# Many-headed attention: scores ahead of the transposed scores, banks exchanged, and queries of two batches in one product

## The chip, the cores and the metric

The kernel runs on one core of a Trainium2 chip. Its engines work side by side and wait for each other only through semaphores: TensorE (PE: products and transposes, written to PSUM; its loads of the stationary operand are listed as PEld), VectorE (DVE), ScalarE (ACT), GpSimd (POOL) and SyncE (SP, which here only issues DMAs). PSUM has eight banks. The metric is the time of one execution on the device in microseconds; the median of several executions is compared.

## The reference

The program is a stack of four gated blocks, each with a cross attention and a feed-forward part, over 32 batches of 112 queries with 256 features and a context of 375 rows. The change touches the cross attention of the third block:

```python
# L2_xattn: 16 heads of 16 features; q = layernorm(x), k = v = ctx
qh = (q @ Wq.T + bq).reshape(B, 112, 16, 16).transpose(0, 2, 1, 3)
kh = (k @ Wk.T + bk).reshape(B, 375, 16, 16).transpose(0, 2, 1, 3)
vh = (v @ Wv.T + bv).reshape(B, 375, 16, 16).transpose(0, 2, 1, 3)
scores = einsum('bhqd,bhkd->bhqk', qh, kh) / sqrt(16)
scores = where(key_padding_mask, scores, -inf)
out = einsum('bhqk,bhkd->bhqd', softmax(scores), vh)
x = x + tanh(g_xattn[2]) * (out.reshape(B, 112, 256) @ Wo.T + bo)
```

## The kernel before

`many_headed_attention` (L2686) computes this attention for 32 batches. A unit is four heads, so a batch has four units and the stage has 128 (n = 4j + u for batch j, unit u). All engines walk the same loop over n from FIRST to LAST. One turn of it is called a slot here; in slot n each engine does what is due for several units at once, in an order fixed by the code.

What happens to a unit:
1. `scores(n)` (L3053, slot n): four heads at once, each on 32 rows of TensorE, 112 queries by 375 keys, written to banks 0 to 3 (SCORE).
2. `find_top(n, h)` on VectorE (L2842), once for each of the four heads: adds the mask and takes the top of each row. `logits_done` counts these.
3. `transpose_top(n)` (L3061, slot n+1) turns the tops, and `extend_q(n)` on VectorE (L2850, slot n+1) writes them into a spare row of the queries, so that the next product comes out with the top subtracted.
4. `scores_t(n)` (L3031, slot n+3): the same scores, transposed, three pieces of 125 keys for four heads, written to banks 4 to 7 (SCORE_T).
5. `exp(n)` on ScalarE (L2935, slot n+3): three instructions for head 0 (bank 4), then three for the other three heads. `probs_done` counts them.
6. `attend(n)` (L3073, slot n+3): probabilities by values.

TensorE does two more things in a slot, each in a bank that the scores leave free for a while.
- The front operation uses bank 4 before the change (FRONT = SCORE_T). It is `transpose_raw` (L3084) in slot u=0, `transpose_att` (L3091) in u=1, `project_out` (L3098) in u=2 and `project_q` of the next batch (L3108) in u=3. It has to wait until the three exponentials of head 0 have read bank 4: `front_free` waits for `probs_done`.
- The back operation uses bank 0 (BACK = SCORE). It is `project_k` (L3120) for half of the next batch's keys in u=0 and u=2, `project_v2` (L3127) with `transpose_xn` (L3133) in u=1, and `project_v01` (L3141) in u=3. `back_free` waits for the first `find_top` of the slot.

Who empties these banks: ScalarE copies keys (L2952), values (L2962, L2966), normalised rows (L2942), raw results (L2973) and `att_t` (L2979); VectorE does `norm_att` (L2855, L2862), `residual` (L2872) and `mask_q` (L2827), which spreads the projected queries of one batch into `q_t` with two instructions.

The order of TensorE in a slot before the change is: transposed scores of n-3, scores of n, front operation, back operation, `transpose_top(n-1)`, `attend(n-3)`. The order of VectorE is: `find_top` for heads 0, 1 and 2, what empties the front operation, `find_top` for head 3, `extend_q(n-1)`, then statistics for a later batch.

Of the kernel before, what the change touches and what calls it, by code (L numbers as in the profile page):

```python
# [13 lines left out]
P = 128  # L14
# [2671 lines left out]
def many_headed_attention(k, w, f):  # L2686
# [3 lines left out]
    with nc.cleanup_on_exit():  # L2690
        V_HOMES = 3
# [11 lines left out]
        xn_t = sb(nc, "xn_t", [P, DC, S], F32)  # L2703
        q_t = sb(nc, "q_t", [P, 2, DC, PARITIES, S], F32)
# [17 lines left out]
        FRONT, BACK = SCORE_T, SCORE  # L2722
# [3 lines left out]
        FIRST, LAST = -UNITS, N + UNITS + 3  # L2726
# [15 lines left out]
        with nc.Block() as block:  # L2742
# [14 lines left out]
            def _(pool):  # L2757
# [30 lines left out]
                norm(0)  # L2788
                mask(0)
# [4 lines left out]
                for n in range(FIRST, LAST):  # L2794
                    j, u = divmod(n, UNITS)
                    if u == 1 and j + 2 < B:
                        norm(j + 2)
# [14 lines left out]
            def _(dve):  # L2812
# [7 lines left out]
                def mask_q(j):  # L2820
                    dve.wait_ge(s["q_done"], j + 1)
                    if j == 0:
                        dve.wait_ge(w.s["scale_ready"], 1)
                    if j >= 2:
                        dve.wait_ge(s["scores_t_done"], UNITS * (j - 1))
                    for a in range(DC):
                        ins = dve.scalar_tensor_tensor(q_t[:, j % 2, a, :, :], k.ps[:, FRONT, a * S:(a + 1) * S].unsqueeze(1).broadcast_to([P, PARITIES, S]),  # L2827
                                                       w.bq[:, a:a + 1], w.q_scale.unsqueeze(2).broadcast_to([P, PARITIES, S]), ALU.add, ALU.mult)
                    ins.then_inc(s["q_masked"], 1)
# [15 lines left out]
                def extend_q(n):  # L2845

                    j, u, a, parity = unit(n)
                    q = q_t[:, j % 2, a, parity, :]
                    dve.wait_ge(s["top_transposed"], n + 1)
                    dve.scalar_tensor_tensor(q, TOP, other[:, parity:parity + 1], q, ALU.mult, ALU.add).then_inc(s["q_extended"], 1)  # L2850
# [23 lines left out]
                statistics(0)  # L2874
                dve.wait_ge(w.s["narrowed"], 2)
# [20 lines left out]
                for n in range(FIRST, LAST):  # L2896
                    j, u = divmod(n, UNITS)
                    if 0 <= n < N:
                        find_top(n, 0)
                        find_top(n, 1)  # L2900
                        find_top(n, 2)
                    if u == 0 and 0 <= j - 2 < B:
                        norm_att(j - 2)
                    if u == 2 and 0 <= j - 2 < B:
                        residual(j - 2)
                    if u == 3 and j + 1 < B:
                        mask_q(j + 1)
# [4 lines left out]
                    if u == 1 and j + 2 < B:  # L2912
                        statistics(j + 2)
                    if u == 2 and 0 <= j - 2 < EARLY:
                        dve.wait_ge(s["residual_done"], j - 1)
                        ternary_statistics(k, f, dve, j - 2)
                    if u == 1 and j == 6:
                        dve.wait_ge(f.s["rows_loaded"], 48)
                        dve.tensor_scalar(f.scale[:, :], f.scale[:, :], 1e-5, None, ALU.max).then_inc(f.s["scale_cut"], 1)
                        dve.wait_ge(f.s["scale_cut"], 1)  # L2920
                        dve.reciprocal(f.inv_scale[:, :], f.scale[:, :]).then_inc(f.s["inverted"], 1)

            @block.scalar
            def _(act):
# [13 lines left out]
                def copy_xn(j):  # L2938
                    act.wait_ge(s["xn_transposed"], j + 1)
                    if j:  # L2940
                        act.wait_ge(s["q_done"], j)
                    act.activation(xn_t[:, :, :], k.ps[:, BACK, D:D + DC * S].rearrange("p (a t) -> p a t", a=DC), ACT.Copy).then_inc(s["xn_t_copied"], 1)  # L2942
# [12 lines left out]
                def copy_v2(j):  # L2955
                    act.wait_ge(s["v2_done"], j + 1)
                    act.wait_ge(s["xn_transposed"], j + 1)
# [22 lines left out]

                for n in range(FIRST, LAST):
                    j, u = divmod(n, UNITS)
                    if 0 <= n - 3 < N:
                        exp(n - 3, 0, 1)
                        exp(n - 3, 1, UNIT)
                    if 0 <= n - 4 < N:
                        copy_raw(n - 4)
                    if u == 1 and 0 <= j - 2 < B:
                        copy_att_t(j - 2)
                    if u == 0 and j + 1 < B:  # L2990
                        copy_k(j + 1, 0)
                    if u == 1 and j + 1 < B:
                        copy_v2(j + 1)
                        copy_xn(j + 1)
# [6 lines left out]
            def _(pe):  # L3001
                def front_free(n):

                    if 0 <= n < N:
                        pe.wait_ge(s["probs_done"], EXPS * n + KC)

                def back_free(n):

                    if 0 <= n < N:
                        pe.wait_ge(s["logits_done"], UNIT * n + 1)  # L3010

                def scores_t(n):
                    j, u, a, parity = unit(n)
                    b, v = divmod(n + 3, UNITS)
# [5 lines left out]
                    if v == 0:  # L3020
                        pe.wait_ge(s["q_masked"], min(b + 1, B))
                    if v == 1 and b >= 2:
                        pe.wait_ge(s["att_normed"], b - 1)
                    if v == 2 and b >= 2:
                        pe.wait_ge(s["att_t_copied"], b - 1)
                    if v == 3 and b >= 2:
                        pe.wait_ge(s["residual_done"], b - 1)
                    for r in range(KC):
                        for h in range(UNIT):
                            rows = slice(h * VW, (h + 1) * VW)  # L3030
                            mm = pe.matmul(k.ps[0:KR, SCORE_T + h, r * S:(r + 1) * S], k_t[rows, j % 2, a, parity, r * KR:(r + 1) * KR],  # L3031
                                           q_t[rows, j % 2, a, parity, :], start=True, stop=True)
                    mm.then_inc(s["scores_t_done"], 1)

                def scores(n):
                    j, u, a, parity = unit(n)
                    pe.wait_ge(s["q_masked"], j + 1)
# [5 lines left out]
                    if u == 0:  # L3043
                        pe.wait_ge(s["v01_copied"], j + 1)
                    if u == 1:
                        pe.wait_ge(s["k_copied"], min(DC * (j + 1) + 1, DC * B))
                    if u == 2:
                        pe.wait_ge(s["xn_t_copied"], min(j + 2, B))
                    if u == 3:
                        pe.wait_ge(s["k_copied"], DC * min(j + 2, B))  # L3050
                    for h in range(UNIT):
                        rows = slice(h * VW, (h + 1) * VW)
                        mm = pe.matmul(k.ps[0:S, SCORE + h, 0:L], q_t[rows, j % 2, a, parity, :], k_t[rows, j % 2, a, parity, :], start=True, stop=True)  # L3053
# [23 lines left out]
                def transpose_raw(j):  # L3077
                    front_free(UNITS * (j + 2) - 3)
                    pe.wait_ge(s["raw_copied"], UNITS * (j + 1))
                    pe.wait_ge(s["q_masked"], min(j + 3, B))  # L3080
# [6 lines left out]
                def transpose_att(j):  # L3087
                    front_free(UNITS * (j + 2) + 1 - 3)
# [5 lines left out]
                def project_out(j):  # L3094
                    front_free(UNITS * (j + 2) + 2 - 3)
# [5 lines left out]
                def project_q(j):  # L3101
                    front_free(UNITS * (j - 1) + 3 - 3)
                    pe.wait_ge(s["xn_t_copied"], j + 1)
                    if j >= 3:
                        pe.wait_ge(s["residual_done"], j - 2)
                    for a in range(DC):
                        for c in range(DC):
                            mm = pe.matmul(k.ps[:, FRONT, a * S:(a + 1) * S], w.wq_t[:, c, a * P:(a + 1) * P], xn_t[:, c, :], start=c == 0, stop=c == DC - 1)  # L3108
                    mm.then_inc(s["q_done"], 1)

                def project_k(j, a):
                    back_free(UNITS * (j - 1) + 2 * a)
                    if a == 0:
                        pe.wait_ge(w.ctx_t_loaded[j % 2], 16 * (j // 2 + 1))
                        if j:
                            pe.wait_ge(s["v01_copied"], j)
                    else:
                        pe.wait_ge(s["xn_t_copied"], j + 1)
# [30 lines left out]
                mm.then_inc(s["gbo_done"], 1)  # L3149
                for n in range(FIRST, LAST):  # L3150
                    j, u = divmod(n, UNITS)
                    if 0 <= n - 3 < N:
                        scores_t(n - 3)
                    if 0 <= n < N:
                        scores(n)
                    if u == 0 and 0 <= j - 2 < B:
                        transpose_raw(j - 2)
                    if u == 1 and 0 <= j - 2 < B:
                        transpose_att(j - 2)
                    if u == 2 and 0 <= j - 2 < B:  # L3160
                        project_out(j - 2)
                    if u == 3 and j + 1 < B:
                        project_q(j + 1)
                    if u == 0 and j + 1 < B:
                        project_k(j + 1, 0)
                    if u == 1 and j + 1 < B:
                        project_v2(j + 1)
                        transpose_xn(j + 1)
# [6 lines left out]
                    if 0 <= n - 3 < N:  # L3175
                        attend(n - 3)
# [492 lines left out]
```

## Time and profile before

| | us |
|---|---|
| median of 3 runs (all: 3018.54, 3021.53, 3033.44) | 3021.53 |
| the profiled execution, its own time | 3033.43 |
| its span, first to last instruction | 3031.7 |
| of it, first to last product of this attention's scores (L3053) | 1972.66 to 2589.33 |
| TensorE busy (share of the span) | 2859.1 (94%) |
| VectorE busy | 1949.8 (64%) |
| ScalarE busy | 1399.9 (46%) |
| GpSimd busy | 648.5 (21%) |

The profile is of one execution. The chain of waits says who released whom; the view in order of time shows instructions of one kind merged into a row with their count, and in square brackets how long the engine had been idle and what ended it. One thing has to be known to read TensorE's rows: products follow each other before the one ahead has ended, so the distance between two starts is what a product costs, not its duration.

### The profile page before, as it was taken

How to read it: one execution, taken by the hardware profiler on the slowest of the kernel's cores; microseconds unless marked ns; L12 is line 12 of the kernel's file. 1: busy time of each engine (PE TensorE's matmuls, PEld its weight loads, DVE VectorE, ACT ScalarE, POOL GpSimd, SP SyncE). 2: the span in 40 equal slices, each digit the busy share in tenths (PEclk: the TensorE clock that was granted, in tenths of full speed). 3: DMA queues.
4: the chain of work that ended last, by engine and by line, in shares of the span. 5: the costliest groups of instructions: out<-in, count | busy, mean ns of one | idle time of the engine just before them, and what ended most of it. 6: DMA issues, size and time to landing. Idle time of an engine off the chain costs nothing. (4 is left out here: it accounts for less than half of the span.)

```text
span 3031.7 us, 64486 instructions
## 1 busy us (share of the span) xinstructions
PE 2859.1 (94%) x24996; PEld 2190.1 (72%) x24996; DVE 1949.8 (64%) x4257; ACT 1399.9 (46%) x3005; POOL 648.5 (21%) x954
## 2 busy tenths in 40 slices
PE   8996999989999999999999999789999999799999
PEld 7873565667789999999999999656666666456444
DVE  5774111138587878787787877656666665489664
ACT  3431111126555555555555555456666666456000
POOL 4565000036200211023001300112212112036000
PEclk9997999989999999999999999999999999799999
DMA  9643223149400000000000000000000000346100
GB/s 303 207 129 109 84 104 125 63 152 278 149 2 1 2 2 2 2 1 2 2 1 2 1 1 2 19 26 23 22 23 22 23 22 12 107 127 212 51 14 21
DMA packets 79680, 185.69 MB, mean 61 GB/s; under 512 B 13111, under 2 KB 23332, under 8 KB 79046
## 3 DMA queue, kind: packets, MB, share of 16 engines
q1 hardware_dynamic: 62838, 141.51, 14.5%
q10 hardware_dynamic: 10208, 25.30, 2.7%
q0 software_dynamic: 6336, 14.76, 1.7%
q8 instruction: 204, 3.34, 0.4%
q14 instruction: 94, 0.77, 0.1%
HBM read 150.27 MB, written 27.79 MB: 59 GB/s over the span
## 5 line engine op out<-in xcount | busy, mean ns | idle before, releaser
L2842 DVE CUSTOM_DVE_ANT_0 masked<-ps,add 112x375 f32<-112x375 f32 x512 | 256.5, 544 | 208.2 <-PE ps L3053 208.2
L2935 ACT ACTIVATE probs_t<-ps,add_t 125x112 f32<-125x112 f32 (+1 forms) x768 | 273.3, 455 | 111.6 <-PE ps L3031 111.6
L1735 DVE TENSOR_TENSOR hidden<-gated,ps 128x512 f32<-128x512 f32 x64 | 44.0, 688 | 298.2 <-PE ps L1778 298.2
L2352 DVE TENSOR_REDUCE top<-ps 112x16 f32<-112x1792 f32 x96 | 194.2, 2023 | 45.5 <-PE ps L2591 45.4
L3517 PE MATMUL ps<-we,xn_t 128*128 128x512 f32 x448 | 203.0, 617 | 0.9 <-PEq L847 0.9
L2368 DVE TENSOR_TENSOR probs<-probs,inv_sum 112x1792 f32<-112x1792 f32 x96 | 198.1, 2063 | 3.3
L2364 DVE TENSOR_REDUCE row_sum<-probs 112x16 f32<-112x1792 f32 x96 | 193.9, 2020 | 4.3 <-ACT probs L2476 4.3
L2356 DVE TENSOR_TENSOR probs<-ps,top 112x1792 f32<-112x1792 f32 x96 | 194.3, 2024 | 3.3
L2559 PE MATMUL ps<-ident,probs 112*112 112x112 f32 x1536 | 179.9, 260 | 8.2 <-ACT probs_t L2471 7.3
L2471 ACT ACTIVATE probs_t<-ps 112x896 f32<-112x896 f32 x192 | 176.0, 917 | 15.1 <-PE ps L2559 3.7
L2550 PE MATMUL ps<-wv,nodes 128*112 128x256 f32 x768 | 181.5, 380 | 0.0
L2559 PEld LDWEIGHTS ps<-ident,probs 112*112 112x112 f32 x1536 | 162.3, 134 | 25.7 <-issue 7.9
L2574 PE MATMUL ps<-nodes,wq 128*128 128x224 f32 x768 | 178.1, 355 | 0.1
L2576 PE MATMUL ps<-att_t,wo 128*128 128x224 f32 x768 | 176.6, 353 | 0.0
L2345 DVE COPY v<-ps 112x512 f32<-112x512 f32 x96 | 66.4, 691 | 167.6 <-PE ps L2550 167.6
L2526 PE MATMUL ps<-nodes,wkh 128*128 128x224 f32 x768 | 172.5, 368 | 0.0
L3517 PEld LDWEIGHTS ps<-we,xn_t 128*128 128x128 f32 x448 | 88.6, 199 | 112.3 <-issue 99.8
L1716 ACT ACTIVATE gated<-ps 128x512 f32<-128x512 f32 x64 | 38.2, 597 | 282.9 <-PE ps L1773 282.9
L2476 ACT ACTIVATE probs<-probs 112x1792 f32<-112x1792 f32 x96 | 162.9, 1697 | 8.3 <-DVE probs L2356 8.2
L2526 PE MATMUL ps<-nodes,wqh 128*128 128x224 f32 x768 | 161.0, 353 | 0.0
L2550 PEld LDWEIGHTS ps<-wv,nodes 128*112 128x112 f32 x768 | 136.2, 177 | 23.3
L2526 PEld LDWEIGHTS ps<-nodes,wkh 128*128 128x128 f32 x768 | 139.0, 192 | 16.5 <-issue 16.1
(471 smaller groups left out, 6098.7 us busy)
## 6 DMA issues: line engine op xcount, KB each, us to landing
ctx_t<-in_ctx_T_dram SPq DMA_DIRECT2D x96, 375.0 KB, 4.3
ctx_sb<-in_ctx_dram ACTq DMA_DIRECT2D x64, 384.0 KB, 4.0
ctx_sb<-in_ctx_dram SPq DMA_DIRECT2D x32, 384.0 KB, 7.6
ctx_sb<-in_ctx_T_dram SPq DMA_DIRECT2D x32, 375.0 KB, 3.0
queue<-zeros SPq DMA_DIRECT2D x32, 256.0 KB, 4.9
rows<-queue SPq DMA_DIRECT2D x16, 512.0 KB, 5.0
outputs<-out SPq DMA_DIRECT2D x16, 512.0 KB, 2.9
mask_in<-in_mask_BxSxS_fk_dram SPq DMA_DIRECT2D x16, 328.1 KB, 7.0
```

The lines of the kernel that those rows point to most:

```text
L2352: dve.tensor_reduce(top[:, :, :], scores, AX.X, ALU.max).then_inc(s["top_done"], 1)
L2356: dve.tensor_tensor(probs[:, m % 2, :, :, :], scores, top[:, :, :].unsqueeze(3).broadcast_to([S, 4, PAIR * HQ, S]), ALU.subtract).then_inc ...
L2364: dve.tensor_reduce(row_sum[:, :, :], p, AX.X, ALU.add).then_inc(s["sum_done"], 1)
L2368: dve.tensor_tensor(p, p, inv_sum[:, :, :].unsqueeze(3).broadcast_to([S, 4, PAIR * HQ, S]), ALU.mult).then_inc(s["probs_normed"], 1)
L2526: mm = pe.matmul(k.ps[:, bank, a * PS:(a + 1) * PS], weights[:, c, i, a * P:(a + 1) * P], node[:, i, :], start=i == 0, stop=i == DC - 1)
L2550: mm = pe.matmul(k.ps[0:S, ODD, b * D:(b + 1) * D], node_v[:, i, b * S:(b + 1) * S], w.wv[:, c, i, :], start=i == 0, stop=i == DC - 1)
L2559: mm = pe.transpose(k.ps[0:S, PT + h // 4, h % 4 * S:(h % 4 + 1) * S], probs[:, m % 2, h % 4, b * HQ + h // 4, :], k.ident[0:S, 0:S])
L2574: pe.matmul(k.ps[:, EVEN, a * PS:(a + 1) * PS], w.wq[:, c, i, cut], node_q[:, i, :], start=i == 0, stop=False)
L2576: mm = pe.matmul(k.ps[:, EVEN, a * PS:(a + 1) * PS], w.wo[:, c, i, cut], att_t[:, i, :], start=False, stop=i == DC - 1)
L2842: dve.tensor_tensor_reduce(out=masked[:, h % 2, :], in0=k.ps[0:S, SCORE + h, 0:L], in1=add[:, j % 2, :], scale=1.0, scalar=HIDE, op0=ALU.a ...
L2935: act.activation(probs_t[:, n % 2, r, first:last, :], k.ps[0:KR, SCORE_T + first:SCORE_T + last, r * S:(r + 1) * S], ACT.Exp, bias=add_t[: ...
L3517: mm = pe.matmul(k.ps[:, Y + at % YB, :], xn_t[:, c, (j + u) * P:(j + u + 1) * P], r.we[:, c, e:e + TWO, :].rearrange("p e d -> p (e d)"), ...
```

## The change

- The banks are exchanged: FRONT is now bank 0, BACK bank 4. `front_free` waits for the slot's first `find_top`, `back_free` for the three exponentials of head 0 of unit n-2.
- TensorE computes `scores(n)` first in a slot and the transposed scores after it. The transposed scores, the exponentials and `attend` now come two slots after the scores, not three, and the loop ends one slot earlier.
- The front operations move one place: `transpose_raw` to u=3 of the batch before, `transpose_att` to u=0, `project_out` to u=1.
- `project_q` is done for two batches at once, four instructions in the program with 224 moving columns instead of 112, in slot u=2 of every odd batch. The even batches have no front operation in u=2. `mask_q` does two batches too, with four instructions. `q_t` holds four batches (Q_HOMES = 4).
- Normalised rows are made one batch earlier. Batch 0's are transposed ahead of the loop, and the first `project_k` waits for their copy.
- The waits that protect the banks follow: `scores` waits for what empties the front operation, `scores_t` for the copies of the back operation.

```diff
-        xn_t = sb(nc, "xn_t", [P, DC, S], F32)
-        q_t = sb(nc, "q_t", [P, 2, DC, PARITIES, S], F32)
+        xn_t = sb(nc, "xn_t", [P, DC, 2, S], F32)
+        q_t = sb(nc, "q_t", [P, DC, Q_HOMES, PARITIES, S], F32)
...
-        FRONT, BACK = SCORE_T, SCORE
+        FRONT, BACK = SCORE, SCORE_T
...
-        FIRST, LAST = -UNITS, N + UNITS + 3
+        FIRST, LAST = -UNITS, N + UNITS + 2
...
+                    for i in range(2):
+                        for a in range(DC):
+                            queries = k.ps[:, FRONT, (2 * a + i) * S:(2 * a + i + 1) * S]
+                            ins = dve.scalar_tensor_tensor(q_t[:, a, home + i, :, :], queries.unsqueeze(1).broadcast_to([P, PARITIES, S]), w.bq[:, a:a + 1],
+                                                           w.q_scale.unsqueeze(2).broadcast_to([P, PARITIES, S]), ALU.add, ALU.mult)
...
                 def front_free(n):
 
                     if 0 <= n < N:
-                        pe.wait_ge(s["probs_done"], EXPS * n + KC)
+                        pe.wait_ge(s["logits_done"], UNIT * n + 1)
 
                 def back_free(n):
 
-                    if 0 <= n < N:
-                        pe.wait_ge(s["logits_done"], UNIT * n + 1)
+                    if 0 <= n - 2 < N:
+                        pe.wait_ge(s["probs_done"], EXPS * (n - 2) + KC)
...
                     if v == 0:
-                        pe.wait_ge(s["q_masked"], min(b + 1, B))
...
+                        pe.wait_ge(s["v01_copied"], min(b + 1, B))
+                    if v == 1:
+                        pe.wait_ge(s["k_copied"], min(DC * (b + 1) + 1, DC * B))
...
+                def project_q(p):
+                    j = 2 * p
+                    front_free(UNITS * (j - 1) + 2)
+                    pe.wait_ge(s["xn_t_copied"], j + 2)
...
                         for c in range(DC):
-                            mm = pe.matmul(k.ps[:, FRONT, a * S:(a + 1) * S], w.wq_t[:, c, a * P:(a + 1) * P], xn_t[:, c, :], start=c == 0, stop=c == DC - 1)
+                            mm = pe.matmul(k.ps[:, FRONT, a * 2 * S:(a + 1) * 2 * S], w.wq_t[:, c, a * P:(a + 1) * P],
+                                           xn_t[:, c, :, :].rearrange("p b t -> p (b t)"), start=c == 0, stop=c == DC - 1)
...
+                transpose_xn(0)
                 for n in range(FIRST, LAST):
                     j, u = divmod(n, UNITS)
-                    if 0 <= n - 3 < N:
-                        scores_t(n - 3)
                     if 0 <= n < N:
                         scores(n)
+                    if 0 <= n - 2 < N:
+                        scores_t(n - 2)
...
+                    if u == 2 and j % 2 and j + 1 < B:
+                        project_q((j + 1) // 2)
+                    if u == 3 and 0 <= j - 1 < B:
+                        transpose_raw(j - 1)
```

The same in TensorE's order. Before, slots u=2 and u=3 of a batch in the middle (L3031 transposed scores, L3053 scores, L3098 output projection, L3120 keys, L3061 tops, L3073 attend, L3108 queries, L3141 values):

```order
L3031 MATMUL ps<-q_t,k_t 125x112 x12
L3053 MATMUL ps<-k_t,q_t 112x375 x4
L3098 MATMUL ps<-ctx_sb,att_t 112x256 x2
L3120 MATMUL ps<-ctx_sb 128x375 x2
L3061 MATMUL ps<-ident,neg_top 128x112
L3073 MATMUL ps<-probs_t,v 32x112 x12
L3031 MATMUL ps<-q_t,k_t 125x112 x12
L3053 MATMUL ps<-k_t,q_t 112x375 x4
L3108 MATMUL ps<-xn_t,ctx_sb 128x112 x4
L3141 MATMUL ps<-ctx_sb 125x256 x4
L3061 MATMUL ps<-ident,neg_top 128x112
```

TensorE after the change, slots u=2 and u=3 of an odd batch (L3062 scores, L3040 transposed scores, L3118 queries of two batches, L3134 keys, L3070 tops, L3082 attend, L3093 raw results, L3155 values):

```order
L3062 MATMUL ps<-k_t,q_t 112x375 x4
L3040 MATMUL ps<-q_t,k_t 125x112 x12
L3118 MATMUL ps<-xn_t,ctx_sb 128x224 x4
L3134 MATMUL ps<-ctx_sb 128x375 x2
L3070 MATMUL ps<-ident,neg_top 128x112
L3082 MATMUL ps<-probs_t,v 32x112 x12
L3062 MATMUL ps<-k_t,q_t 112x375 x4
L3040 MATMUL ps<-q_t,k_t 125x112 x12
L3093 MATMUL ps<-ident,att_raw 112x128 x4
L3155 MATMUL ps<-ctx_sb 125x256 x4
L3070 MATMUL ps<-ident,neg_top 128x112
```

The transposed scores moved behind the scores, the query product (now 224 columns) from u=3 to u=2 beside the keys, and the values lost it as their neighbour.

VectorE before, from head 0's top of slot u=3 to the extended queries (L2842 find the top, L2827 `mask_q`, L2850 `extend_q`):

```order
L2842 ISA masked,neg_top<-ps,add 112x375
L2842 ISA neg_top 112x1
L2842 ISA masked,neg_top<-ps,add 112x375
L2842 ISA neg_top 112x1
L2842 ISA masked,neg_top<-ps,add 112x375
L2842 ISA neg_top 112x1
L2827 SCALAR_TENSOR_TENSOR q_t<-ps,ctx_sb 128x224 x2
L2842 ISA masked,neg_top<-ps,add 112x375
L2842 ISA neg_top 112x1
L2850 SCALAR_TENSOR_TENSOR q_t<-ps,other,q_t 128x112
```

VectorE after, the same stretch of slot u=2 of an odd batch (L2847, L2832 and L2855 are the same three):

```order
L2847 ISA masked,neg_top<-ps,add 112x375
L2847 ISA neg_top 112x1
L2847 ISA masked,neg_top<-ps,add 112x375
L2847 ISA neg_top 112x1
L2847 ISA masked,neg_top<-ps,add 112x375
L2847 ISA neg_top 112x1
L2832 SCALAR_TENSOR_TENSOR q_t<-ps,ctx_sb 128x224 x4
L2847 ISA masked,neg_top<-ps,add 112x375
L2847 ISA neg_top 112x1
L2855 SCALAR_TENSOR_TENSOR q_t<-ps,other,q_t 128x112
```

`mask_q` grew from two instructions to four ahead of the last `find_top` of its slot, and stands in every eighth slot instead of every fourth.

## Rows read from the trace of the kernel before

**Rows 1.** Busy time of the engines, from the page.
```profile
PE 2859.1 (94%) x24996; PEld 2190.1 (72%) x24996; DVE 1949.8 (64%) x4257; ACT 1399.9 (46%) x3005; POOL 648.5 (21%) x954
```

**Rows 2.** Waits in the stage: who waited, for whom, us in total, times, longest.
```profile
PEld ps L3084 <- ACT probs_t L2935: 31.6, 31, 1.3
```

**Rows 3.** Order of time, one slot: start, us, engine, line, operation, count, [idle before].
```profile
2208.98 0.92 PE L3031 MATMUL ps<-q_t,k_t 32*125 32x112 f32 x24
2209.72 0.82 PE L3053 MATMUL ps<-k_t,q_t 32*112 32x375 f32 x8
2210.03 2.14 ACT L2935 ACTIVATE probs_t<-ps,add_t 125x112 f32<-125x112 f32 x6 [0.53 <-PE ps L3031]
2210.60 0.55 DVE L2842 CUSTOM_DVE_ANT_0 masked<-ps,add 112x375 f32<-112x375 f32 x1 [1.71 <-PE ps L3053]
2210.92 0.20 PEld L3091 LDWEIGHTS ps<-ident,att 112*128 112x128 f32 x2 [1.00 <-ACT probs_t L2935]
2211.21 0.72 PEld L3127 LDWEIGHTS ps<-ctx_sb 128*125 128x125 f32 x4
2212.38 0.26 PE L3061 MATMUL ps<-ident,neg_top 112*128 112x112 f32 x1
2212.56 0.54 PEld L3073 LDWEIGHTS ps<-probs_t,v 125*32 125x32 f32 x24
2213.27 0.74 PEld L3031 LDWEIGHTS ps<-q_t,k_t 32*125 32x125 f32 x24 [0.17 <-issue]
```

**Rows 4.** Order of time: starts of slot u=0 of two batches in a row.
```profile
2204.38 0.74 PEld L3031 LDWEIGHTS ps<-q_t,k_t 32*125 32x125 f32 x24 [0.17 <-issue]
2223.91 0.74 PEld L3031 LDWEIGHTS ps<-q_t,k_t 32*125 32x125 f32 x24 [0.17 <-issue]
```

**Rows 5.** Order of time: slot n=2, which has no transposed scores.
```profile
1980.91 0.32 PEld L3053 LDWEIGHTS ps<-k_t,q_t 32*112 32x112 f32 x8 [0.95 <-issue]
1981.90 0.55 DVE L2842 CUSTOM_DVE_ANT_0 masked<-ps,add 112x375 f32<-112x375 f32 x1 [0.80 <-PE ps L3053]
1982.51 0.93 PEld L3120 LDWEIGHTS ps<-ctx_sb 128*128 128x128 f32 x4 [1.28 <-DVE neg_top L2842]
1983.88 0.26 PE L3061 MATMUL ps<-ident,neg_top 112*128 112x112 f32 x1
1984.08 0.67 ACT L2952 ACTIVATE k_t<-ps,k_bias,own 128x375 f32<-128x375 f32 x1 [3.28 <-PE ps L3120]
```

**Rows 6.** Order of time: queries, values and masked queries in a slot u=3.
```profile
2200.75 0.97 PEld L3108 LDWEIGHTS ps<-xn_t,ctx_sb 128*128 128x128 f32 x8 [1.00 <-ACT probs_t L2935]
2201.64 1.59 PEld L3141 LDWEIGHTS ps<-ctx_sb 128*125 128x125 f32 x8
2201.94 0.81 DVE L2827 SCALAR_TENSOR_TENSOR q_t<-ps,ctx_sb 128x224 f32<-128x224 f32 x2
2202.66 0.54 DVE L2842 CUSTOM_DVE_ANT_0 masked<-ps,add 112x375 f32<-112x375 f32 x1
2203.48 0.26 PE L3061 MATMUL ps<-ident,neg_top 112*128 112x112 f32 x1
```

**Rows 7.** Order of time: products with 224 moving columns, an earlier stage.
```profile
1939.85 0.92 PE L2576 MATMUL ps<-att_t,wo 128*128 128x224 f32 x4
1940.61 0.92 PE L2574 MATMUL ps<-nodes,wq 128*128 128x224 f32 x4
```

**Rows 8.** Order of time: a slot at the end in which only the exponentials hold up `attend`.
```profile
2592.87 2.14 ACT L2935 ACTIVATE probs_t<-ps,add_t 125x112 f32<-125x112 f32 x6 [1.75 <-PE ps L3031]
2595.12 0.57 PEld L3073 LDWEIGHTS ps<-probs_t,v 125*32 125x32 f32 x24 [0.83 <-issue]
```

**Rows 9.** Order of time: the warm-up, normalised rows of batch 0.
```profile
1960.74 1.23 POOL L2767 TENSOR_SCALAR xn<-x_sb,mean_var,rstd 112x256 f32<-112x256 f32 x1
```

**Rows 10.** Order of time: starts of slots u=0 of batches 1 and 2 (cut by the view's window).
```profile
1989.89 0.64 PEld L3031 LDWEIGHTS ps<-q_t,k_t 32*125 32x125 f32 x20 [0.17 <-issue]
2008.77 0.61 PEld L3031 LDWEIGHTS ps<-q_t,k_t 32*125 32x125 f32 x17 [0.17 <-issue]
```

More of the change, by code:

```diff
@@ L2690, in many_headed_attention @@
     with nc.cleanup_on_exit():
-        V_HOMES = 3
+        V_HOMES, Q_HOMES = 3, 4
         w.pad = sb(nc, "pad", [S, B * L], U8)
@@ L2788, in _ @@
                 norm(0)
+                norm(1)
                 mask(0)
@@ L2795, in _ @@
                     j, u = divmod(n, UNITS)
-                    if u == 1 and j + 2 < B:
-                        norm(j + 2)
+                    if u == 2 and j + 3 < B:
+                        norm(j + 3)
                     if u == 2 and 0 < j + 1 < B:
@@ L2818, in statistics, with mask_q @@
                     dve.bn_aggr(mean_var[:, j % 2, :], stats[:, j % 2, :]).then_inc(s["mean_done"], 1)
-                def mask_q(j):
-                    dve.wait_ge(s["q_done"], j + 1)
-                    if j == 0:
+                def mask_q(p):
+                    home = 2 * p % Q_HOMES
+                    dve.wait_ge(s["q_done"], p + 1)
+                    if p == 0:
                         dve.wait_ge(w.s["scale_ready"], 1)
[L2824 to L2828, printed above, removed]
+                    if p >= 2:
+                        dve.wait_ge(s["scores_t_done"], UNITS * 2 * (p - 1))
+                    for i in range(2):
[3 more added lines that the diff above has]
+                                                           w.q_scale.unsqueeze(2).broadcast_to([P, PARITIES, S]), ALU.add, ALU.mult)
                     ins.then_inc(s["q_masked"], 1)
@@ L2874, in _ @@
                 statistics(0)
+                statistics(1)
                 dve.wait_ge(w.s["narrowed"], 2)
@@ L2901, in _ @@
                         find_top(n, 2)
-                    if u == 0 and 0 <= j - 2 < B:
-                        norm_att(j - 2)
-                    if u == 2 and 0 <= j - 2 < B:
+                    if u == 1 and 0 <= j - 2 < B:
                         residual(j - 2)
-                    if u == 3 and j + 1 < B:
-                        mask_q(j + 1)
+                    if u == 2 and j % 2 and j + 1 < B:
+                        mask_q((j + 1) // 2)
+                    if u == 3 and 0 <= j - 1 < B:
+                        norm_att(j - 1)
                     if 0 <= n < N:
@@ L2911, in _ @@
                         extend_q(n - 1)
-                    if u == 1 and j + 2 < B:
-                        statistics(j + 2)
+                    if u == 1 and j + 3 < B:
+                        statistics(j + 3)
                     if u == 2 and 0 <= j - 2 < EARLY:
@@ L2993, in _ @@
                         copy_v2(j + 1)
-                        copy_xn(j + 1)
+                    if u == 1 and j + 2 < B:
+                        copy_xn(j + 2)
                     if u == 2 and j + 1 < B:
@@ L3031, in scores_t @@
                             mm = pe.matmul(k.ps[0:KR, SCORE_T + h, r * S:(r + 1) * S], k_t[rows, j % 2, a, parity, r * KR:(r + 1) * KR],
-                                           q_t[rows, j % 2, a, parity, :], start=True, stop=True)
+                                           q_t[rows, a, j % Q_HOMES, parity, :], start=True, stop=True)
                     mm.then_inc(s["scores_t_done"], 1)
@@ L3042, in scores @@
                         pe.wait_ge(s["q_extended"], n - 1)
[L3043 to L3048, printed above, removed]
+                    if u == 0 and j >= 2:
+                        pe.wait_ge(s["att_normed"], j - 1)
+                    if u == 1 and j >= 2:
+                        pe.wait_ge(s["att_t_copied"], j - 1)
+                    if u == 2 and j >= 2:
+                        pe.wait_ge(s["residual_done"], j - 1)
                     if u == 3:
-                        pe.wait_ge(s["k_copied"], DC * min(j + 2, B))
+                        pe.wait_ge(s["q_masked"], min((j + 1) // 2 + 1, B // 2))
                     for h in range(UNIT):
                         rows = slice(h * VW, (h + 1) * VW)
-                        mm = pe.matmul(k.ps[0:S, SCORE + h, 0:L], q_t[rows, j % 2, a, parity, :], k_t[rows, j % 2, a, parity, :], start=True, stop=True)
+                        mm = pe.matmul(k.ps[0:S, SCORE + h, 0:L], q_t[rows, a, j % Q_HOMES, parity, :], k_t[rows, j % 2, a, parity, :], start=True, stop=True)
                     mm.then_inc(s["scores_done"], 1)
@@ L3087, in transpose_att @@
                 def transpose_att(j):
-                    front_free(UNITS * (j + 2) + 1 - 3)
+                    front_free(UNITS * (j + 2))
                     pe.wait_ge(s["att_normed"], j + 1)
@@ L3116, in project_k @@
                             pe.wait_ge(s["v01_copied"], j)
-                    else:
-                        pe.wait_ge(s["xn_t_copied"], j + 1)
+                        else:
+                            pe.wait_ge(s["xn_t_copied"], 1)
+                    else:
+                        pe.wait_ge(s["v2_copied"], j + 1)
+                        pe.wait_ge(s["xn_t_copied"], min(j + 2, B))
                     for c in range(DC):
@@ L3167, in _ @@
                         project_v2(j + 1)
-                        transpose_xn(j + 1)
+                    if u == 1 and j + 2 < B:
+                        transpose_xn(j + 2)
                     if u == 2 and j + 1 < B:
@@ L3174, in _ @@
                         transpose_top(n - 1)
-                    if 0 <= n - 3 < N:
-                        attend(n - 3)
+                    if 0 <= n - 2 < N:
+                        attend(n - 2)
 MAX_INT = 127.0
```

53 lines of the change are left out of this document (24 added, 29 removed).

## The prediction

> **What bounds the kernel now.** I read the page's busy times first, then the list of waits of this stage, then single slots in order of time. TensorE is busy 94% of the span, VectorE 64%, ScalarE 46% [rows 1]. That makes TensorE the engine to watch, but its busy time counts overlapping products, so I work with the distances between starts. A batch takes 2223.91 - 2204.38 = 19.53 us [rows 4], very regularly, and a slot's length is set by a loop through TensorE, ScalarE and back. The list of waits shows it: the front operation waits for the exponentials in every batch [rows 2], 31 times for one of the four, and the others read alike.
>
> I count from a slot's first load. In the slot of [rows 3], the shortest of the four, the transposed scores start at 0, the scores at 0.74, ScalarE's exponentials at 1.05 (2210.03), and the front operation is let in at 1.94 (2210.92), 0.89 after the exponentials began. The scores alone would have left TensorE free at about 0.74 + 2 x 0.316 = 1.37. So some 0.57 us of each slot is a real hole. (0.316 is the distance between two products of 375 columns: from the first load to the product behind the four of them is 1983.88 - 1982.51 = 1.37 [rows 5], less about 0.1 for the first load, by four.) From the front operation on, TensorE is closed up: back operation, tops, `attend`, next slot.
>
> **Part 1: scores first, banks exchanged.** The new slot can be put together from rows, since one slot of the warm-up already runs in the new order [rows 5]: scores from 0, first `find_top` at 0.99, and the operation behind it let in at 1.60.
> - Scores: two rounds of four products, 0.32 each behind a first load of 0.1, so the transposed scores start at about 0.75. They run six rounds; in [rows 3] ScalarE starts 1.05 after their first load, of which about 0.09 is that first load's delay. ScalarE starts at 0.75 + 0.96 = 1.71.
> - Front operation: in at 1.60 instead of 1.94, a gain of 0.34.
> - Back operation: waits for three exponentials of head 0, and so starts at 1.71 + 0.89 = 2.60 at the earliest. Before, it came right behind the front operation. This is the wait that takes the place of the removed one, and it is later, because the whole of the scores (0.75) now stands ahead of the transposed scores that feed ScalarE.
> - `attend`: not before 1.71 + 2.14 + 0.11 = 3.96; the 0.11 is 2595.12 less the end of the exponentials at 2595.01 [rows 8].
>
> Everything from the back operation to the next slot is then: keys 1.37 to the tops [rows 5], the values' two thirds 1.84 (2203.48 - 2201.64, [rows 6]), values' last third with normalised rows 1.17 (2212.38 - 2211.21, [rows 3]); tops to `attend` 0.18 and `attend` to the next slot 0.71 [rows 3]. New slots:
> - u=0: 2.60 + 1.37 + 0.89 = 4.86 or 4.87
> - u=1: 2.60 + 1.17 + 0.89 = 4.66; with `attend` held to 3.96, 4.67
> - u=2, even batch, no front operation: 4.87
> - u=3: 2.60 + 1.84 + 0.89 = 5.33 (5.34)
>
> That is 19.76 for an even batch, against 19.53: 0.23 slower. The front operations fit into the gap between 1.60 and 2.60: the longest that is left, the output projection, has four passes of 256 columns, 0.1 + 4 x 0.22 = 0.98 by the values' eight in 1.84. So they are hidden, but the gap is as long as they were.
>
> **Part 2: queries of two batches.** Saved: one of two query products in u=3. Added: in u=2 of odd batches eight passes of 224 columns ahead of the keys. The distance of such passes is (1940.61 - 1939.85)/4 = 0.19 [rows 7], so the product ends at 1.70 + 8 x 0.19 = 3.21, beyond 2.60, and no longer fits the gap. TensorE alone would need 3.21 + 4 x 0.316 + 0.89 = 5.37. VectorE is later still: the last pass starts at 3.02, is done about 0.42 later (duration 0.92 - 3 x 0.19 plus 0.06), and only then can `mask_q` begin, at 3.44. One instruction of it costs (2202.66 - 2201.94)/2 = 0.36 [rows 6], four cost 1.44, and head 3's `find_top` (0.55) stands behind them: 3.44 + 1.44 + 0.55 + 0.05 = 5.48. The next slot's scores need it. Queued behind it are `extend_q` and some statistics, which end before the next slot's first `find_top` at 5.48 + 0.99. So an odd batch takes 19.76 + 5.48 - 4.87 = 20.37, 0.84 slower.
>
> The Trainium skill, page "TensorE: Matmul & The Clock Gate", section "Part 2: What happens when you issue a matmul", has one column enter the array per cycle, so a pass of 224 columns would cost 93 ns. The row shows 0.19, twice that. By the page the queries would end near 2.6, the odd slot would shrink to the even one's 4.87, and the whole sum would come to about +8; I go by the row.
>
> **Test of the method.** Batch 1 has no front operation but in u=3, so three of its slots wait for VectorE. In the old order the first `find_top` starts 1.62 into a slot [rows 3], the back operation 0.61 later, at 2.23: slots of 2.23 + 1.37 + 0.89 = 4.49, 4.29, 4.49 and, with the queries' 0.89 (2201.64 - 2200.75, [rows 6]), 1.94 + 0.89 + 1.84 + 0.89 = 5.56, in all 18.83. Measured is 2008.77 - 1989.89 = 18.88 [rows 10]. After the change it is an odd batch of 20.37.
>
> **The edges.** The transposed scores come one slot earlier. At the end that saves a slot of 4.04 us, but the last batch's four slots grow from 4.04 to 4.67 since `attend` waits until 3.96: -1.5 to -3, I take -2.5. At the start the first keys wait for batch 0's normalised rows (ready at 1961.97 [rows 9]), their transposes and copy, about 2 us; then queries and keys stand in a row before ScalarE's copy, 1.6 more, and the slower clock there can add 1. The first scores slip by some 4.5 us, and the first two slots, which no longer wait for ScalarE, give back about 3 less 1.7 that slot 2 loses. That is +2.5, with ends 0 and +6.
>
> **The sum.** Batch 1: +1.5. Batches 2 to 30: 15 even at +0.23 = 3.5, 14 odd at +0.84 = 11.8. Edges 0. In all +16.8; I say +16.5. The profiled execution took 3033.43, so its like would be 3050. It is the slowest of the three shown; their median is 3021.53, and the forecast is 3038. All else in the program is untouched.
>
> What I put at nothing: ScalarE's key copy in u=0. It starts 1.57 after the keys [rows 5], at 4.17, and takes 1.22, so it ends 0.52 into the next slot, where the transposed scores need it at about 0.6. The cover is less than 0.1 us. Bounds: 0, and 0.15 for two slots in a batch.
>
> **The rivals.**
> 1. *The odd slot is cheaper.* If the queries or `mask_q` overlap more than I think, an odd batch costs like an even one. For it: only an estimate says when `mask_q` may start. Against: both rows are clean. 29 x 0.23 + 0.9 for batch 1 = +8, time 3030, no change that can be told.
> 2. *The key copy is late.* The transposed scores of u=1 and u=3 wait 0.15 each for ScalarE, and everything behind slides: 0.3 x 31 = +9 on top, +26, time 3047. For it: the small cover. Against: the old order had the same small cover and shows no wait.
> 3. *The back wait is hidden, faster.* If transposed scores could run between the rounds of the scores and not behind them, the exponentials would start about 0.6 earlier and the back operation at 2.0, right behind the front operation. Then each slot gains the 0.34 of the front operation, and the pair of queries about 0.3: 31 x (1.4 + 0.3) = -53, time 2969. It decides from a start of the exponentials before about 1.4. Against: in [rows 3] the transposed scores and scores stand 0.74 apart, all four row groups are used by both.
>
> **How the numbers follow.** Forecast 0.58, rival 1 0.24, rival 2 0.11, rival 3 0.07. This kernel's runs tell changes over about 0.5%, 15 us, from none. The forecast of +16.5 lies just beyond, and some of its own range (from +11 to +22 with the edges and the rounding of 0.03 a slot) falls within: of its 0.58, 0.38 slower and 0.20 same. Slower: 0.38 + 0.11 = 0.49. Same: 0.20 + 0.24 = 0.44. Faster 0.07. The range takes in rivals 1 and 2: 3025 to 3052.
>
> **What would show it.** In the new trace: exponentials 1.71 after a slot's first load, front operation at 1.60, back operation at 2.60 with a wait for `probs_t`, slots of 4.87, 4.67, 4.87 or 5.48, and 5.34, and batches that alternate between 19.8 and 20.4. Waits of the key, value or row loads for `probs_t`, 31 of each, replace those of the front operations. The forecast is wrong if the back operation starts well before 2.5, if odd and even batches are alike, or if a wait of the transposed scores for `k_t` shows up.

## The result and the profile after

The changed kernel takes 3048.2 us (median of 4, 3042.9 to 3049.6), the kernel before 3020.0 (4 runs): 1.0069 times as long, 95% interval 1.0044 to 1.0094. That ratio makes it about 21 us slower (13 to 28); the medians lie 28 apart. The forecast was slower by 16.5. The two profiled spans differ by 14.2 only (3045.9 and 3031.7), since the profiled execution of before was the slowest of its four and lost some 10 us in stages that the change doesn't touch (3 ahead of this one, 7 behind it). So the comparison is made within the stage, from its first load (L3148 before, L3162 after) to the end of its last residual:

| us | before | after | difference | forecast |
|---|---|---|---|---|
| first load to the start of batch 1 | 30.77 | 36.12 | +5.4 | +2.5 |
| batch 1 | 18.88 | 20.70 | +1.8 | +1.5 |
| batches 2 to 30 | 566.88 | 586.28 | +19.4 | +15.3 |
| batch 31 to the last residual | 36.85 | 34.47 | -2.4 | -2.5 |
| stage | 653.38 | 677.57 | +24.2 | +16.8 |

The busy times of the page say nothing of it; the row that answers to [rows 1]:

```profile
PE 2867.4 (94%) x24868; PEld 2202.2 (72%) x24868; DVE 1947.1 (64%) x4257; ACT 1398.5 (46%) x3005; POOL 648.1 (21%) x954
```

The waits of the stage (us in total, times, longest) show what took the place of [rows 2]:

```profile
PEld ps L3134 <- ACT probs_t L2941: 43.4, 46, 1.5
...
PEld ps L3155 <- ACT probs_t L2941: 19.3, 31, 1.1
...
PEld ps L3141 <- ACT probs_t L2941: 10.5, 30, 1.2
...
PE ps L3062 <- ACT k_t L2958: 6.9, 15, 0.5
...
PEld ps L3093 <- DVE neg_top L2847: 5.9, 31, 0.2
```

The front operations (L3093 stands for them) now wait 0.2, and the back operations wait for the exponentials instead: keys in 46 of 62 slots (those beside paired queries need not), values in 31 and 30. The row of L3062 is new and was not in the forecast's sum: 15 scores start 0.45 late, one in each odd batch. The view puts that down to `k_t`; it will turn out to be VectorE.

A slot u=2 of an even batch in order of time (start, us, engine, line), answering to [rows 3]:

```profile
2143.88 0.29 PEld L3062 LDWEIGHTS ps<-k_t,q_t 32*112 32x112 f32 x8 [0.17 <-issue]
...
2145.55 2.13 ACT L2941 ACTIVATE probs_t<-ps,add_t 125x112 f32<-125x112 f32 x6 [1.73 <-PE ps L3040]
...
2146.45 0.93 PEld L3134 LDWEIGHTS ps<-ctx_sb 128*128 128x128 f32 x4 [1.20 <-ACT probs_t L2941]
```

The exponentials start 1.67 into the slot (forecast 1.71), the keys 2.57 (2.60), and TensorE's loads stand still for 1.20 before them. The slots of an even batch are, u=0 to u=3, 4.84, 4.69, 4.84 and 5.33; forecast were 4.87, 4.67, 4.87 and 5.34.

The same slot of an odd batch, with the queries of two batches:

```profile
2123.18 0.29 PEld L3062 LDWEIGHTS ps<-k_t,q_t 32*112 32x112 f32 x8 [0.17 <-issue]
...
2124.76 1.43 PEld L3118 LDWEIGHTS ps<-xn_t,ctx_sb 128*128 128x128 f32 x8 [0.22 <-DVE neg_top L2847]
...
2126.37 1.43 PE L3134 MATMUL ps<-ctx_sb 128*128 128x375 f32 x4
...
2126.57 1.53 DVE L2832 SCALAR_TENSOR_TENSOR q_t<-ps,ctx_sb 128x224 f32<-128x224 f32 x4 [0.94 <-PE ps L3118]
...
2127.83 0.54 PEld L3082 LDWEIGHTS ps<-probs_t,v 125*32 125x32 f32 x24 [0.36 <-issue]
...
2128.02 0.54 DVE L2847 CUSTOM_DVE_ANT_0 masked<-ps,add 112x375 f32<-112x375 f32 x1
...
2128.48 0.33 DVE L2855 SCALAR_TENSOR_TENSOR q_t<-ps,other,q_t 128x112 f32<-128x112 f32 x1
...
2129.04 0.32 PEld L3062 LDWEIGHTS ps<-k_t,q_t 32*112 32x112 f32 x8 [0.67 <-issue]
```

The first product of the keys starts at 3.19 (forecast 3.21), `mask_q` at 3.39 (3.44), head 3's `find_top` at 4.84 (4.88). `attend` is over TensorE at 2127.83 + 0.71 = 2128.54, but the next scores load at 2129.04: the slot takes 5.86, not 5.48. They start 0.23 after `extend_q` (L2855) ended at 2128.81.

### The profile page after: what moved, and what is told of

Its sections match the earlier page's. It is cut to its first block and busy times, and to the rows that moved or that the text cites. A ratio compares the mean times of both kernels' runs of the same rounds, so it can differ in the third digit from the quotient of the medians.

```text
span 3045.9 us, 64199 instructions
## 1 busy us (share of the span) xinstructions
PE 2867.4 (94%) x24868; PEld 2202.2 (72%) x24868; DVE 1947.1 (64%) x4257; ACT 1398.5 (46%) x3005; POOL 648.1 (21%) x954
## 5 line engine op out<-in xcount | busy, mean ns | idle before, releaser
L2847 DVE CUSTOM_DVE_ANT_0 masked<-ps,add 112x375 f32<-112x375 f32 x512 | 255.3, 544 | 138.3 <-PE ps L3062 138.3
L2471 ACT ACTIVATE probs_t<-ps 112x896 f32<-112x896 f32 x192 | 176.0, 917 | 15.1 <-PE ps L2559 3.7
```

The costliest lines, as they stand in the source:

```text
L2847: dve.tensor_tensor_reduce(out=masked[:, h % 2, :], in0=k.ps[0:S, SCORE + h, 0:L], in1=add[:, j % 2, :], scale=1.0, scalar=HIDE, op0=ALU.a ...
```

## The experiments

Two theories. The first, the prediction's: a slot is a loop scores, transposed scores, exponentials, back operation, and what TensorE does before 2.6 us is free. The second: TensorE, busy 94%, sets the time by its amount of work. "Batches" below is the time from the start of batch 2 to that of batch 31, in the profiled execution: 566.88 before, 586.28 after.

**`mask_q` behind head 3's `find_top`** (in the changed kernel).

```diff
-                    if u == 2 and j % 2 and j + 1 < B:
-                        mask_q((j + 1) // 2)
                     if u == 3 and 0 <= j - 1 < B:
                         norm_att(j - 1)
                     if 0 <= n < N:
                         find_top(n, 3)
+                    if u == 2 and j % 2 and j + 1 < B:
+                        mask_q((j + 1) // 2)
```

> The changed kernel, with mask_q of the odd batches behind head 3's find_top and ahead of extend_q. Theory (VectorE's queue sets the odd slot: mask_q, find_top, extend_q in a row, then the scores' waits): find_top of head 3 then runs while TensorE still makes the queries, mask_q ends at 4.84 after the slot's first load, extend_q at 5.17, and the slot takes 5.40 instead of 5.86; odd batches 20.25 instead of 20.70, even ones 19.69 as now, in all -7 us against the changed kernel, about 3041. Rival (TensorE's own work with 224 columns, or the key copy, sets the odd slot): 5.86 stays, no difference.

Measured 3038.7 (its slowest run, 3040.9, lies below the changed kernel's fastest, 3042.9), batches 580.21, odd batches 20.25; the stage is 5.3 shorter, where 7 was expected. Its odd slot, in order of time:

```profile
2121.13 0.29 PEld L3062 LDWEIGHTS ps<-k_t,q_t 32*112 32x112 f32 x8 [0.17 <-issue]
...
2124.53 1.53 DVE L2832 SCALAR_TENSOR_TENSOR q_t<-ps,ctx_sb 128x224 f32<-128x224 f32 x4 [0.47 <-PE ps L3118]
...
2125.97 0.33 DVE L2855 SCALAR_TENSOR_TENSOR q_t<-ps,other,q_t 128x112 f32<-128x112 f32 x1
...
2126.52 0.32 PEld L3062 LDWEIGHTS ps<-k_t,q_t 32*112 32x112 f32 x8 [0.20 <-issue]
```

The slot is 5.39, as expected, though TensorE and the key copy do the same work. VectorE's queue had set the 5.86. The next scores again start 0.22 after `extend_q`, but here that is no second measurement of a wait: TensorE's loads stand still for only 0.20 before them, against 0.17 in slots where nothing holds them up. So TensorE and VectorE are ready at nearly the same time, and a still shorter queue of VectorE would gain next to nothing.

**The pairing alone undone** (order, banks and early rows stay).

```diff
-                    if u == 2 and j % 2 and j + 1 < B:
-                        project_q((j + 1) // 2)
+                    if u == 2 and j + 1 < B:
+                        project_q(j + 1)
...
```

`project_q` and `mask_q` do one batch each here, and the waits on them count accordingly.

> The changed kernel with the pairing alone undone: queries of one batch, 112 columns, in u=2 of every batch, mask_q with two instructions; order, banks and early rows as changed. Theory (the queries of one batch fit into the gap before the back operation, those of two do not): all batches alike, slots 4.84, 4.69, 4.84, 5.33, 19.69 a batch; -1.01 in 15 batches and about 1 us less at the start, -16 us against the changed kernel, about +5 against the kernel before. Rival (the pairing saves TensorE time and the order costs more than it shows): twice as many loads of queries, 0.35 a batch more, +11 against the changed kernel.

Measured 3035.1, 1.0048 (1.0033 to 1.0064) of before; batches 572.48, every one 19.71. TensorE issues more passes, and the kernel's median is 13 us below that of the changed one. The batches came as expected, the total did not: about +5 against the kernel before was expected, and the timed ratio gives +14.5, the stage (664.06) +10.7. One part of the miss is the stretch from batch 31 to the last residual, which took 38.59 against 34.47 in the changed kernel although nothing was changed there; the granted clock was at its lower level in it from 2601.4 to 2604.8 and from 2608.2 on.

**Order and banks alone** (single queries, and rows normalised at the old time).

```diff
-                    if u == 1 and j + 2 < B:
-                        transpose_xn(j + 2)
+                    if u == 1 and j + 1 < B:
+                        transpose_xn(j + 1)
...
-                transpose_xn(0)
                 for n in range(FIRST, LAST):
```

The statistics, the normalised rows and the waits on them go back to the old time in the same way.

> As the single queries, and the normalised rows again made at the time of the kernel before (batch 0's inside the loop, no wait of the first keys for them). What is left of the change is the order, the banks and the places of the front operations. Theory: slots as with the single queries, 19.69; the first scores come 3 to 4.5 us earlier than in the changed kernel, since the first keys need not wait and TensorE's clock rises sooner. Stage -19 to -20 against the changed kernel, and +2 to +4 against the kernel before (5 from the batches, less 2.5 at the end, plus about 1 at the start). Rival: the late start comes from the order itself (queries ahead of the second keys); then the start is as late as with the single queries.

Measured 3028.0, 1.0024 (1.0014 to 1.0034) of before; batches 571.91, stage 657.52, +4.1 against before. First load to first scores is 13.6, as before (13.5), against 19.6 in the changed kernel and 16.8 with single queries. So the late start came half from the early rows (3.2) and half from the paired queries (2.8), not from the order; 3 to 4.5 in all was expected, and it was 6.0. The clock moves with both: it is at 2.4 GHz 15.4 us after the first load in the changed kernel, 12.1 with single queries, and 5.2 here and before.

**The pairing alone, in the old order** (the edit as against the kernel before; `mask_q`, the early rows and the waits follow the changed kernel).

```diff
-                    if u == 3 and j + 1 < B:
-                        project_q(j + 1)
+                    if u == 3 and j % 2 and j + 1 < B:
+                        project_q((j + 1) // 2)
```

> The kernel before with the pairing alone: queries of two batches in one product in u=3 of every odd batch, mask_q with four instructions, normalised rows one batch earlier; order and banks as before. Theory (a pair costs what its place costs): an even batch's u=3 has no front operation and waits for the first find_top, 2.23 + 1.84 + 0.89 = 4.96 instead of 5.57; an odd one's grows by 224 against 112 columns, 1.94 + 1.61 + 1.84 - 0.1 + 0.89 = 6.2; half of the sum is 5.58, so the batches cost nothing. With the early rows' later start, +3 to +5 us against the kernel before. Rival (the pairing in itself costs 1 us per odd batch, wherever it stands): +15 and the start, about +19.

Measured 3025.5, 1.0005 (0.9995 to 1.0014) of before; batches 565.90, alternating 18.92 and 20.15. The slots with and without queries, by their first loads:

```profile
2126.69 0.74 PEld L3039 LDWEIGHTS ps<-q_t,k_t 32*125 32x125 f32 x24 [0.17 <-issue]
...
2128.64 1.43 PEld L3118 LDWEIGHTS ps<-xn_t,ctx_sb 128*128 128x128 f32 x8 [1.00 <-ACT probs_t L2941]
2130.07 1.67 PEld L3155 LDWEIGHTS ps<-ctx_sb 128*125 128x125 f32 x8
...
2132.88 0.29 PEld L3039 LDWEIGHTS ps<-q_t,k_t 32*125 32x125 f32 x6 [0.17 <-DVE q_t L2855]
...
2146.84 0.74 PEld L3039 LDWEIGHTS ps<-q_t,k_t 32*125 32x125 f32 x24 [0.17 <-issue]
...
2149.08 1.59 PEld L3155 LDWEIGHTS ps<-ctx_sb 128*125 128x125 f32 x8 [1.29 <-DVE neg_top L2847]
...
2151.81 0.31 PEld L3039 LDWEIGHTS ps<-q_t,k_t 32*125 32x125 f32 x8 [0.17 <-issue]
```

6.19 and 4.97, expected 6.2 and 4.96, together as much as two slots of 5.57: in the loop the pair itself costs nothing, only its place does. In this profile batch 1 starts 8.6 later than before, counted from the stage's first load; the granted clock had fallen back to 1.2 GHz from 1982.4 to 1992.6, in the middle of batch 0, which no other profile here shows. The timed runs show +1.5 in all (expected +3 to +5), so how much the start costs in most runs stays open.

**More transposes, changed kernel and kernel before** (raw twice, `att` three times, the same result).

```diff
-                    for u in range(UNITS):
+                    for _ in range(2):
+                        for u in range(UNITS):
...
-                    for a in range(DC):
+                    for _ in range(3):
+                        for a in range(DC):
```

> The changed kernel with transpose_raw done twice and transpose_att three times in a row (the same result), 0.4 + 0.4 us more of TensorE's work a batch, in u=3 and u=0. Theory (front operations lie in the gap between 1.60 and 2.60): u=0 has 0.29 + 0.4, u=3 0.8, both end before 2.6; nothing changes, 0 to +2 us against the changed kernel. Rival (TensorE's work sets the time, it is 94% busy): +0.8 a batch, +25 us.

> The kernel before with the same additional transposes, in u=0 and u=1, where the front operation starts at 1.94 and all of TensorE's work behind it is closed up. Theory: every added transpose is paid, about 0.8 a batch, 31 batches, +25 us against the kernel before. Rival (in the old order too a wait behind the front operation hides them): no difference.

In the changed kernel: 3048.6, batches 586.19 against 586.28, no difference. In the kernel before: 3045.6, 1.0069 (1.0051 to 1.0088), batches 587.14, 0.70 more in each (0.8 was expected, and +25 us in all; the ratio gives +21). A slot u=0 of each, with the added transposes; the changed kernel first, then the kernel before:

```profile
2136.84 0.29 PEld L3062 LDWEIGHTS ps<-k_t,q_t 32*112 32x112 f32 x8 [0.17 <-issue]
...
2138.41 0.59 PEld L3102 LDWEIGHTS ps<-ident,att 112*128 112x128 f32 x6 [0.21 <-DVE neg_top L2847]
...
2139.40 0.93 PEld L3136 LDWEIGHTS ps<-ctx_sb 128*128 128x128 f32 x4 [0.40 <-ACT probs_t L2941]
...
2141.67 0.29 PEld L3062 LDWEIGHTS ps<-k_t,q_t 32*112 32x112 f32 x8 [0.17 <-issue]
```

```profile
2111.33 0.74 PEld L3031 LDWEIGHTS ps<-q_t,k_t 32*125 32x125 f32 x24 [0.17 <-issue]
...
2113.28 0.84 PEld L3085 LDWEIGHTS ps<-ident,att_raw 128*112 128x112 f32 x8 [1.01 <-ACT probs_t L2935]
2114.10 0.93 PEld L3122 LDWEIGHTS ps<-ctx_sb 128*128 128x128 f32 x4
...
2116.37 0.74 PEld L3031 LDWEIGHTS ps<-q_t,k_t 32*125 32x125 f32 x24 [0.17 <-issue]
```

In the first the keys wait 0.40 all the same and start at 2.56; in the second they follow the transposes without a gap, and the slot grew from 4.60 to 5.04. The same edit is free in one order and paid in the other. The theory of TensorE's amount of work falls.

**Part of the values moved into the gap** (on top of order and banks alone).

```diff
+                def project_v0(j):
+                    front_free(UNITS * j)
+                    for c in range(DC):
+                        mm = pe.matmul(k.ps[0:KR, FRONT, D:2 * D], w.ctx_t[j % 2][:, c, 0:KR], w.wv_t[:, c, :], start=c == 0, stop=c == DC - 1)
+                    mm.then_inc(s["v0_done"], 1)
...
+                    if u == 0 and 0 <= j < B:
+                        project_v0(j)
                     if u == 0 and 0 <= j - 2 < B:
                         transpose_att(j - 2)
```

> As the order and banks alone, and the first third of the values' projection moved from the back operation of u=3 to the front operation of u=0, ahead of transpose_att, where TensorE waits for the exponentials. Theory (work ahead of 2.60 is free, work behind it is paid): u=3 shrinks from 5.33 to 4.69, where attend's own wait for the exponentials is the bound, u=0 grows from 4.84 to 5.02; 19.23 a batch instead of 19.69, -14 us against the order alone and about -10 against the kernel before, near 3010. Rival (TensorE's amount of work sets a batch): the same work in another place, 19.69 stays.

Measured 3009.4 (11 runs), 0.9973 (0.9962 to 0.9984) of before: some 8 us faster than the kernel before (about 10 expected), and faster than the changed one. Batches 560.60, each 19.32: slots 4.99, 4.80, 4.84, 4.70. Slot u=3 lost the 0.63 expected. Slot u=1 is 0.09 longer than before the move, which was not expected: in u=0 ScalarE now copies that third of the values ahead of the keys, and the transposed scores of u=1, which wait for the keys' copy, load at 0.73 instead of 0.41:

```profile
2102.33 0.44 ACT L2972 ACTIVATE v<-ps 125x256 f32<-125x256 f32 x1
...
2102.60 1.29 ACT L2954 ACTIVATE k_t<-ps,k_bias,own 128x375 f32<-128x375 f32 x2
...
2103.27 0.31 PEld L3065 LDWEIGHTS ps<-k_t,q_t 32*112 32x112 f32 x8 [0.24 <-issue]
...
2104.00 0.77 PEld L3041 LDWEIGHTS ps<-q_t,k_t 32*125 32x125 f32 x24 [0.41 <-issue]
...
2105.96 0.72 PEld L3142 LDWEIGHTS ps<-ctx_sb 128*125 128x125 f32 x4 [0.38 <-ACT probs_t L2937]
...
2108.06 0.29 PEld L3065 LDWEIGHTS ps<-k_t,q_t 32*112 32x112 f32 x8 [0.17 <-issue]
```

The copy of the keys (L2954) ends at 2103.89, and the transposed scores load 0.11 later. That is the forecast's rival 2, the late key copy. It did not come true in the changed kernel (slots u=1 and u=3 are as forecast); its thin cover was used up here.

## Why the prediction was right, and where its terms were off

- **The new wait of the back operation.** Right: 2.57 against 2.60, even batches 19.69 against 19.76. Order and banks alone lose 0.17 a batch. The added transposes showed the gap itself: with them in it, the keys of a slot u=0 still start at 2.56.
- **Front operations free in the gap.** Right, shown by the added transposes.
- **The odd slot.** The mechanism was right (VectorE behind the queries of two batches, not TensorE), the term was too small: 5.48 forecast, 5.86 measured, 0.38 in 15 slots, 5.7 us. The step that was mis-sized is "The next slot's scores need it": they need `find_top`, but also `q_extended` of the unit just extended, a wait that stood in the kernel before too, and I named `extend_q` only as queued behind. That is one more instruction of VectorE (it ends 0.25 after `find_top`), and then 0.23 from its end to the load, where I had put 0.05: 4.84 + 0.54 + 0.25 + 0.23 = 5.86. `mask_q` one place later gave back 0.47 a slot, as this reading says.
- **The start.** Forecast +2.5, measured +5.4. The forecast's terms, 4.5 less 3 plus 1.7, make 3.2 and not 2.5, and two of them were off. The first two slots gave back 1.9 (3.05 and 3.31, before 4.50 and 3.75), not 3; slot 2 lost the 1.7 as forecast, and slot 3 gave back 0.6, which the forecast did not have. The first scores came 6.1 later, not 4.5: the part of the clock, put at 1, was too small. The granted clock of the start is below (windows of the changed kernel, then of the kernel before; the last columns are the clock, the share of the DMA engines and GB/s). It stood at 1.2 GHz for the first 15.4 us, where before it had been at 2.4 GHz after 5.2. The paired queries ran at the low level and took about twice as long as in a batch (loads 1967.50 to 1970.28, 2.78 us, against 1.43), and so did the loads of the values' last third (1.34, against 0.72 before). The two together cost 2.0 more.

```profile
1956.00:1971.40 15.40, 11.84 (x26) 7.44 (x27) 8.40 (x22) 2.21 (x5) 8.27 (x14) 0.50 0.31 89
1971.50:1975.70 4.20, 2.89 (x11) 1.68 (x10) 0.92 (x3) 1.22 (x2) 0.00 (x0) 1.00 0.00 0
...
1959.10:1964.20 5.10, 4.52 (x8) 2.42 (x8) 4.18 (x13) 0.49 (x1) 2.05 (x3) 0.50 0.89 252
1964.40:1975.00 10.60, 7.37 (x37) 4.91 (x38) 4.69 (x13) 2.98 (x6) 4.25 (x8) 1.00 0.14 37
```

- **The end.** -2.4 against -2.5, but the match is luck. The forecast's own working (a slot of 4.04 saved, four slots longer by 0.63) gives -1.5; I took -2.5. And the clock, which the forecast left out here, fell to 1.2 GHz in this stretch in both kernels: before from 2599.2 on, after from 2602.9 to 2606.4, from 2623.4 to 2626.8 and from 2630.3 on. Two slots of batch 31 took 5.23 and 5.60 around the first of these falls, where 4.67 was forecast and 4.66 is what they took in the run with added transposes, whose clock did not fall there. In the five profiles of this order with the values left whole, the stretch took 33.3 to 38.6. So one profile can neither confirm nor refute this term.
- **The rivals.** A cheap odd slot and a hidden back wait did not come; the alternation of 19.69 and 20.70 and the waits for `probs_t` speak against both. By the Trainium skill's one column per cycle (page "TensorE: Matmul & The Clock Gate", section "Part 2: What happens when you issue a matmul") the estimate was that the queries end near 2.6 (1.70 and eight passes of 0.093 make 2.44, still within the gap). Here eight passes of 224 columns take 1.61 (2124.76 to 2126.37), 0.20 each, so that the keys behind them start 3.19 into the slot, and the trace is again at about twice the page's figure.
- **Nearly luck.** A forecast of +16.5 stood hardly outside the noise of 15 us, and terms of 3 to 6 us decided on which side of it the change would fall. The two that were off by most, the odd slot and the start, happened to err in the same direction, away from "no change". The forecast's sum was 4 short of the difference by the ratio, 7 short of the stage's and 11 short of that of the medians.

## What to carry to other kernels

In a loop that passes between engines, ask of each operation on which side of the last wait it stands: here work in front of it was free up to the gap's length, and work behind it was paid nearly in full, and a busy share of 94% does not tell the two apart. Taking the wait off one operation is worth nothing if the next one then waits longer for the same producer. Sharing work over two turns of a loop makes one turn long and the other short; it pays only if the short turn can use the time.

## What the runs showed of the hardware

**From a producer's end to the load that waits for it.** In the odd slots the scores load 0.23 us after `extend_q` ended (2128.81 to 2129.04), and a front operation 0.06 after the end of its `find_top` (2124.70 to 2124.76). The scores stand behind more waits than the front operation, but that this makes the difference was not tried, and one pair of rows of the kernel before speaks against it. There the transposed scores, which stand behind four waits, load 0.08 after `extend_q` ended at 2208.90, though TensorE's loads had stood still for only 0.17 there:

```profile
2208.57 0.33 DVE L2850 SCALAR_TENSOR_TENSOR q_t<-ps,other,q_t 128x112 f32<-128x112 f32 x1
2208.98 0.74 PEld L3031 LDWEIGHTS ps<-q_t,k_t 32*125 32x125 f32 x24 [0.17 <-DVE q_t L2850]
```

**TensorE's clock after a pause.** All nine profiles have 8.7 us without loads for TensorE ahead of the stage's first load, and in that pause the granted clock falls to 1.2 GHz. From that first load to 2.4 GHz it took 5.0 to 5.2 us in the four kernels that make batch 0's normalised rows inside the loop (the kernel before, with and without added transposes, order and banks alone, and values split). It took 12.1 us with the early rows and single queries, and 15.1 to 15.5 us in the four kernels with the early rows and paired queries. Why the early rows go with a later return of the clock was not tried. TensorE's products were busy for 11.84 of the 15.40 us at the low level in the changed kernel, and for 4.52 of 5.10 us in the kernel before.
